# Two batches' cluster logits as extra columns of the dense product, with new instruction orders on every engine

## The reference

```python
x = x + attn_a(layernorm(x))   # stage 1: x @ ((w1'w2) * sparse mask) + b2, then gelu
x = x + ffn(layernorm(x))      # stage 2
x = x + attn_b(layernorm(x))   # stage 3: one-head attention, width 128, biases
x = x + ffn(layernorm(x))      # stage 4, same weights as stage 2

def ffn(x):
    dots = softmax(x @ centroids.T / 0.1)     # 64 clusters
    hits = dots > 0.01
    query_sel = any(hits, axis=1)             # per token
    cluster_sel = any(hits, axis=0)           # over all 2048 tokens
    row_sel = cluster_sel[assignments]        # per output column
    dense = x @ weight.T + bias
    return where(query_sel[:, None] & row_sel[None, :], dense, 0)
```

## Time and profile before

| what | value |
|---|---|
| median of 3 runs | 275.45 us |
| profiled execution | 275.24 us, of which span 273.4 us |
| PE busy | 268.8 us, 98% of the span |
| DVE, ACT, POOL busy | 192.2, 177.0, 163.8 us |
| granted TensorE clock | 0.999 of full |
| PE's share of the chain that ended last | 96% |

### The profile page before, as it was taken

The page is one execution under the profiler, slowest core; times in us unless marked ns, Lnnn a source line. Parts: engine busy times, 40 slices in busy tenths (PEclk is TensorE's granted clock), DMA queues, the critical chain, the costliest instruction groups (busy, mean ns, idle before and its releaser), DMA issues.

```text
span 273.4 us, 4428 instructions
## 1 busy us (share of the span) xinstructions
PE 268.8 (98%) x1397; PEld 225.6 (82%) x1397; DVE 192.2 (70%) x406; ACT 177.0 (65%) x359; POOL 163.8 (60%) x196
## 2 busy tenths in 40 slices
...
DMA packets 10247, 18.25 MB, mean 67 GB/s; under 512 B 1200, under 2 KB 1968, under 8 KB 10224
## 3 DMA queue, kind: packets, MB, share of 16 engines
...
q10 hardware_dynamic: 1440, 2.49, 2.5%
...
## 4 chain that ended last, share of the span: by engine, by line
PE 96%; DMA 1%; DVE 1%; POOL 1%; issue 0%; ACT 0%; DVEq 0%; POOLq 0%
PE m_bank L1018 76%; PE t_bank L1113 12%; PE m_bank L1197 6%; PE t_bank L1119 1%; DMA x_tok<-in_L_attn_a_x 1%; PE m_bank L1073 1%; ACT xn_odd L613 0%; PE t_bank L1138 0%; DVE st L817 0%; POOL rstd L471 0%; POOL ve L470 0%; DVE y_tok L988 0%; DVE x_tok L994 0%; PE m_bank L1144 0%; PE t_bank L1124 0%
## 5 line engine op out<-in xcount | busy, mean ns | idle before, releaser
L1018 PE MATMUL m_bank<-ffn_hi,even_hi 128*128 128x512 f32 x96 | 38.9, 406 | 0.0
L1018 PE MATMUL m_bank<-ffn_lo,even_hi 128*128 128x512 f32 x96 | 37.6, 392 | 0.0
L1018 PE MATMUL m_bank<-ffn_hi,even_lo 128*128 128x512 f32 x96 | 37.4, 390 | 0.0
L602 ACT ACTIVATE ones_and_squares<-x_tok,mv 128x512 bf16<-128x512 f32 x44 | 31.6, 717 | 4.1 <-DVE x_tok L921 3.7
L559 POOL TENSOR_TENSOR y_tok<-y_tok,x_tok 128x512 f32<-128x512 f32 x12 | 15.3, 1289 | 25.6 <-ACT y_tok L755 25.6
L539 POOL TENSOR_TENSOR y_tok<-y_tok,bias_f 128x512 f32<-128x512 f32 x16 | 20.6, 1295 | 16.2 <-ACT y_tok L696 16.2
L467 POOL TENSOR_SCALAR ve<-mv 128x1 f32<-128x1 f32 (+1 forms) x20 | 5.3, 264 | 37.9 <-ACT ones_and_squares L602 36.9
L824 DVE TENSOR_TENSOR even_lo<-t_bank,even_hi 128x512 fp32r<-128x512 f32 x24 | 16.2, 684 | 12.8 <-ACT even_hi L645 12.6
L471 POOL TENSOR_TENSOR rstd<-ve,half 128x1 f32<-128x1 f32 (+1 forms) x31 | 23.5, 758 | 2.6
L824 DVE TENSOR_TENSOR odd_lo<-t_bank,odd_hi 128x512 fp32r<-128x512 f32 x28 | 18.8, 686 | 6.4 <-ACT odd_hi L645 6.2
L1018 PE MATMUL m_bank<-odd_hi,wqkv_hi 128*128 128x512 f32 (+1 forms) x60 | 21.5, 358 | 0.0
...
## 6 DMA issues: line engine op xcount, KB each, us to landing
...
out<-x_tok ACTq DMA_DIRECT2D x8, 256.0 KB, 2.2
out<-x_tok SPq DMA_DIRECT2D x7, 256.0 KB, 2.2
x_tok<-in_L_attn_a_x SPq DMA_DIRECT2D x4, 256.0 KB, 4.1
w_raw<-in_L_attn_a_w SPq DMA_DIRECT2D x4, 256.0 KB, 5.0
xt_other<-in_L_ffn_weight SPq DMA_DIRECT2D x4, 256.0 KB, 5.9
y_tok<-in_L_attn_a_sparse_mask SPq DMA_DIRECT2D x4, 256.0 KB, 6.5
```

The source lines that it names most:

```text
L602: act.activation(squares, x_tok[:, n, :], ACT.Square, bias=sum_of(*key), scale=-float(D), accum_out=mv[:, i, 1:2]).then_inc(done[kind], 1)
L1018: ins = pe.matmul(bank, a, w, start=(first and n == 0), stop=(last and n == count - 1))
```

## The change

For batches 0 and 1 of stage 2 (`MERGED`) the cluster logits are no longer a product of their own. The centroids' columns are stored in front of the dense weight (`cf_hi`, `cf_lo`), and the 64 + 512 = 576 columns are cut in two halves of `WIDE = 288`. A new step `dw2.b.t.h` makes one half of one tile: 12 matmuls of 288 columns, tokens stationary. It can't be cut into chunks, has a PSUM bank of its own, and waits for all four `flo` (the dense weight's low part) and for the split centroids. `evw2` (ACT) copies a half out with the row scale, so the logits come out with tokens on partitions; `cl2`, `lgev`, `tc`, `logit` are gone for these two batches. POOL's `bias2` becomes two instructions there. In all other batches the softmax now works in the PSUM bank of the transposed logits (`choice_in`), and that bank is freed by `prob` instead of `logit`. `prob` computes the reciprocal twice, once to PSUM and once to SBUF. `WARM` goes from 12 to 10, one more load is issued by ACT, and all lists of steps are rewritten.

```diff
-WARM = 12
+WARM = 10
+MERGED = {(2, 0), (2, 1)}
+WIDE = (NC + D) // 2
...
+        cf_hi = sb("cf_hi", [P, KC, 2 * NC + D], F32R)
+        cf_lo = sb("cf_lo", [P, KC, NC + D], F32R)
+        cen_lh, cen_hi, cen_lo = cf_hi[:, :, 0:2 * NC], cf_hi[:, :, NC:2 * NC], cf_hi[:, :, 0:NC]
+        ffn_hi, ffn_lo = cf_hi[:, :, 2 * NC:], cf_lo[:, :, NC:]
+        wide = {2: w2_raw, 4: xt_other}
...
+                elif kind in ("bias2", "bias4") and (int(kind[4]), key[0]) in MERGED:
...
+                    pool.wait_ge(*done_at(f"evw{stage}", (b, t, 0)))
+                    pool.tensor_tensor(y_tok[:, n, 0:D - WIDE], wide[stage][:, t, NC:WIDE], bias_f[:, 0:D - WIDE], ALU.add)
+                    pool.wait_ge(*done_at(f"evw{stage}", (b, t, 1)))
+                    pool.tensor_tensor(y_tok[:, n, D - WIDE:D], y_tok[:, n, D - WIDE:D], bias_f[:, D - WIDE:D],
+                                       ALU.add).then_inc(done[kind], 1)
...
+                elif kind in ("evw2", "evw4"):
...
+                    dst = y_tok[:, n, D - WIDE:D] if h else wide[stage][:, t, 0:WIDE]
+                    act.activation(dst, bank_of(f"dw{stage}", *key)[:, 0:WIDE], ACT.Identity,
+                                   scale=rstd[:, i:i + 1]).then_inc(done[kind], 1)
...
-                    link(dve.reciprocal(crec[:, :], csum[:, :]))
+                    dve.reciprocal(crec[:, :], total).then_inc(shared, 1)
+                    link(dve.reciprocal(share, total))
...
-            freed_by = {"T": "lo", "tc": "logit", "bestT": "csel", "last": "mask_attn", "y1": "x1", "dn2": "ev2",
+            freed_by = {"T": "lo", "tc": "prob", "bestT": "csel", "last": "mask_attn", "y1": "x1", "dn2": "ev2",
...
+                    if kind in ("dw2", "dw4"):
+                        t, h = key[1:]
+                        cols, wides = slice(t * P, (t + 1) * P), slice(h * WIDE, (h + 1) * WIDE)
+                        hi, lo = clustered_in(b)
+                        if kind == "dw2":
+                            pe.wait_ge(*done_at("flo"))
+                            pe.wait_ge(*split("cen", 0, [0]))
+                        pe.wait_ge(*split("x" + kind[2], b, [t]))
+                        ins = products(bank[:, 0:WIDE], [((hi[:, c, cols], lo[:, c, cols]),
+                                                          (cf_hi[:, c, NC:][:, wides], cf_lo[:, c, wides])) for c in range(KC)])
...
 PE_ORDER = """
-dn4.2.3.c3 dn4.3.0.c31 bestT.4 dn4.3.2.c2 tmask.4 masks.4 dn4.3.2.c031 dn4.2.2.c0123 dn4.3.1.c0123 dn4.2.0.c0123
-dn4h.3.3.0 dn4h.3.3.1
...
+dn4.3.1.c1 dn4.3.2.c0 dn4.3.1.c3 dn4.2.0.c3 dn4.3.1.c2 dn4.3.2.c13 dn4.3.1.c0 dn4h.3.3.0 dn4.2.0.c1 dn4h.3.3.1
+dn4.2.0.c02
```

More of the change, by code:

```diff
@@ L39 @@
[L39 to L53, removed]
@@ L130 @@
 SP_ORDER = """
[L131 to L134 removed]
+load.x0.3 load.w2.0 load.w1.1 load.x0.2 load.w2.2 load.x0.0 load.w2.1 load.w2.3 load.sparse.0 load.w1.3
@@ L135 @@
+load.ffn.2 load.w1.2 load.ffn.0 load.ffn.1 load.cen load.sparse.1 load.sparse.2 load.ffn.3 load.sparse.3 load.b2
+load.x.1 load.x.2 load.xt.1 load.x.3 load.xt.3 load.small load.xt.2 load.bias load.late store.0.1 store.1.2
+store.1.1 store.0.2 store.2.1 store.3.1 storeh.3.3.1 store.2.0
 """
-AQ_ORDER = "load.w1.0"
 AS_ORDER = """
-store.0.0 store.1.0 store.0.3 store.1.3 store.3.0 store.2.3 store.3.2 storeh.3.3.0 store.2.2
+store.0.0 store.3.0 store.2.2 store.0.3 store.1.0 store.1.3 storeh.3.3.0 store.3.2 store.2.3
@@ L143 @@
+"""
+AQ_ORDER = """
+load.w1.0 load.x0.1
 """
@@ L701, in _ @@
                     act.wait_ge(*done_at("lmax", key))
+                    if key in MERGED:
+                        for k in range(TPB):
+                            ins = act.activation(ce[:, k, :], wide[stage][:, k, 0:NC], ACT.Exp, bias=ncmx[:, k:k + 1])
+                        ins.then_inc(done[kind], 1)
+                        continue
                     for k in range(TPB):
-                        ins = act.activation(ce[:, k, :], cl[:, k, :], ACT.Exp, bias=ncmx[:, k:k + 1],
+                        ins = act.activation(choice_in(*key)[0][:, k, :], cl[:, k, :], ACT.Exp, bias=ncmx[:, k:k + 1],
                                              scale=rstd[:, i + k:i + k + 1])
```

282 lines of the change are left out of this document (175 added, 107 removed).

## The result

The changed kernel takes 276.75 us, the median of 5 runs (276.28 to 276.90), against 275.45 (275.22 to 275.65) for the kernel before. The ratio is 1.0045, with a 95% interval of 1.003 to 1.006: slower by about half a per cent. The forecast was 276.1, with a range of 274.7 to 277.5. The profiled execution took 276.75 us, its span 274.9.

A forecast was written before the change was run, and what follows sets the result against it. PE's matmul stream was taken as the bound, busy 98% of the span; -0.45 (stream) - 0.7 (waits) + 0.4 (slips) + 0.4 (start) + 1.1 (end) = +0.75 us gave 276.1 us, range 274.7 to 277.5.

The forecast's parts named there:

- Stream: PE's matmul stream: merge and orders -0.45 us, waits that go -0.7, slips +0.4.
- The three waits: PE's waits at `tc.4.2`, `tc.4.3` and `tmask.4`, 0.24 us each, all to go: -0.7 us.
- slips: New waits on shortened paths such as `pv.0` and `T.x2.3.3`: +0.4 us, bounds 0 and +2.
- Start: Up to `last.0`, held to 13.7 us by a late w1 load, one transpose group owed: +0.54, taken as +0.4 us.
- if nothing is late: Start: condition on PE's own work putting `last.0` at 12.6 us, before the w1 load was considered.
- End: After PE's last start, a whole tile last instead of a half: +1.1 us, bounds +0.6 and +1.9.
- The first two terms: End: DVE's first pass to the copy 0.85 us instead of 0.59, the copy 0.77 instead of 0.44.
- I cost these at nothing.: ACT's wide copies (at most +1.9 us a batch), DVE's tiny reciprocal and POOL's 8 more instructions, hidden by idle time: nothing.
- A: Start: `last.0` not held by its load, -0.5 in place of +0.4, no slips: 274.9 us; chance 0.18.
- D: Merge does what it says, start at 0, end at +0.6: 275.3 us; chance 0.18.
- B: Stream: 288-column matmuls at the Trainium skill's smaller cost on top, time 0.8 lower, 275.3 us; chance 0.05.
- C: Body: a new wait over 1 us, at a `dw2` bank or a shortened path: 277.5 us; chance 0.17.

The follow-up runs named there:

- Experiments 2 to 4: Changed kernel: 2, 12 warm-ups and w1 loads earlier, 276.61 us; 3, 10 warm-ups, those loads and `cstat` later, 276.61; 4, whole start of before, 12 warm-ups, 275.83.
- experiment 5: Changed kernel with the end of before on PE, DVE and SP, 276.96 us; then ACT's half store also behind POOL's two, 276.64 us.
- experiment 7: Changed kernel with the unmerged batches' softmax in SBUF instead of the PSUM bank, `tc`'s bank freed by `logit`: 278.29 us.
- experiment 8: Kernel before, its order kept on every engine, with batch 1 alone merged and the softmax in SBUF: 281.50 us, ratio 1.0189.

## Why the prediction was right, and where not

The direction and the range were right, and the sum was 0.65 us short.

- **Stream.** Right in sum. 288 columns at 0.1329 was forecast, 0.1329 measured in the rows above (0.134 over all of them). The three waits went, `tc.2.3` kept its own. Forecast -0.75, measured -0.80, but with luck: by distances the two new waits are 0.8 and 0.2 us, 1.0 where 0.4 was put for slips, at places that weren't named, so the rest of the stream came out 0.6 better than its terms. No run shows the merge alone in the new order, so how the -0.80 divides between it and the orders stays open.
- **Start.** The step that failed: "I take +0.4 and keep -0.5 and +1.1 as bounds", measured +1.45, outside them. I followed one load, `w1.2`, and got the end of its split nearly right (13.7, measured 13.99), and the transpose group "still owed" too (0.46 for 0.44). But `last.0` came at 14.59. What I left out is the clause "if nothing is late" in front of it: `norm.1.0.1` stood behind two splits that wait for loads, and held `attn.1` to 11.30 to 11.51 in the profiles at full pace; in the changed kernel's own profile PE's slow first products held it to 11.76, and the pace isn't in the prediction at all. Experiments 2 to 4 show three bounds one behind the other, loads, DVE's wait for the centroids, POOL's sums. Taking one away brought `y1.0.0.c0` forward by 0.4 us and the time by 0.1 at most; putting the whole start back gave 0.8 to 1.4.
- **End.** Forecast +1.1 from PE's last start, measured +0.96 (4.41 against 3.45), but experiment 5 shows the reason to be partly another one. The first two terms, 0.26 + 0.33, came as 0.66 up to SP's last issue. The third, 0.5 for a whole tile's store against a half's, came as 0.3, and not for that reason: a half landed no sooner there. I took the later `tmask.4` to cost nothing because DVE had room. DVE had; that the DMA engines had not is what the full slices and the landing times point to, and no run thinned out those stores.
- **"I cost these at nothing."** Right for the merge's copies. For the softmax in the bank it was right by luck: I counted "a tiny reciprocal", while experiment 7 shows that this edit keeps 1.5 us away in the new order.
- **Rivals.** A (the start gains) and D (the ends cancel) are out, since start and end each lost. B (the small cost on top) is out by the 0.1329. C (a new wait of over 1 us) didn't come in the changed kernel, but did in experiment 8, and there at 2.55 us.
